# Which engine copies the transposed attention weights out of PSUM: a transformer layer with a 1024-token sliding window on eight NeuronCores

## The chip, the cores and the metric

One Trainium2 chip (trn2), all eight NeuronCores, one program on each. The metric is the device time in microseconds of the slowest core, as the median of several executions. Two batches of 4096 tokens are split into eight pieces of 1024 tokens; each core computes its own piece and reads another 1024 tokens in front of it (the halo) for keys and values. There is no exchange between cores. Engines are called PE (matmul), ACT (ScalarE), DVE (VectorE), POOL (GpSimd, which here only issues the casting DMAs) and SP.

## What is computed

The reference, cut to what matters:

```python
# attention: 32 query heads, 8 kv heads, head size 128, window 1024
q = rope(x @ wq); k = rope(x @ wk); v = x @ wv
scores = einsum('bqhgd,bshd->bhgqs', q, k) * 128 ** -0.5
scores = where((j <= i) & (j > i - 1024), scores, neg)
attn   = softmax(scores)
x = layernorm(x + einsum('bhgqs,bshd->bqhgd', attn, v) @ wo)
# ffn: dense 4096x4096 plus bias, plus the LoRA rank picked per token by a gate
x = layernorm(x + x @ W.T + b + lora(x))
```

## The kernel before, in words

The program of a core goes through four stages, in this order: keys and values of 2048 tokens (L382 and its helpers); then twice (`NPASS`, two passes of 512 tokens) the attention of all 32 heads followed by the output projection, the first layer norm and a transposition (L739 to L798); then the dense layer of the ffn (L939 and after). All matmuls are bf16.

`Prog.do` records one group of instructions for one engine and derives its waits from `Res` objects: a resource remembers the last writer's token (`w`) and the readers since (`r`). A read waits for `w`; a write waits for `w` and for every reader. Each engine executes its own list strictly in the order in which the program text recorded it. Nothing is reordered later.

The attention of one pass walks over heads h and, inside a head, over four query blocks s4 of 128 rows. A query block looks at KW = 1152 keys (nine blocks of 128). One block, called a step below, is spread over three turns of the loop:

- `emit_C` (L599 and after): the scores on PE, in three pieces of 512, 512 and 128 columns (all L613) with two mask matmuls (L618, L622), into three PSUM banks: 0 to 2 or 3 to 5 by the parity of the step.
- `emit_post`: one exp over the 1152 columns on ACT (L628, whose accumulator is read by a second instruction), then on DVE the sum's correction (L632), the reciprocal (L635) and the scaling of the probabilities `pb` (L637).
- `tailT`, one turn later: nine PE transposes of `pb`. Eight go to bank 6 (L647), the ninth (L654) into the free end of the third score bank of this step's parity. Then two copies bring them to SBUF as `pts`: eight blocks in one copy of 1024 columns (L658), the ninth in a copy of 128 columns (L663). Both declare `r_pts` as written.
- `tailA`, one turn after that: nine matmuls of V against `pts` (L676), whose 128x128 result ACT copies away (L681).

Between these stands `emit_A_piece`: eight of the 32 matmuls that project the next head's queries (L554, bank 7). At the end of a head `emit_B` turns the projected queries into rotated ones: ACT copies bank 7 to `qraw` (L565), PE multiplies by a permutation (L568), DVE does two products and a sum (L575, L578, L581). The first score matmul of the next head needs the result.

A turn of the loop thus reads: scores of i, `tailA` of i-2, projection piece, exp and scaling of i, `tailT` of i-1. After the last head, `tailsA` and `tailsT` are emptied, and the loads of the residual rows (`xo`) and of the output weights (`wo_r`) feed the next stage; the `xo` loads are released by the last projection piece.

```python
                    post, tT, tA = emit_C(h, s4)
                    if len(tailsA) >= 2:
                        tailsA.pop(0)()
                    if h + 1 < HQ:
                        emit_A_piece(h + 1, s4, QS)
                    post()
                    if tailsT:
                        tailsT.pop(0)()
```

Of the kernel before, what the change touches and what calls it, by code (L numbers as in the profile page):

```python
# [9 lines left out]
AF = mybir.ActivationFunctionType  # L10
# [144 lines left out]
def build_program(cfg):  # L155
# [36 lines left out]
    with contextlib.ExitStack() as es:  # L192
# [75 lines left out]
        def bankb(i):  # L268
            return PSb[:, i * 1024:(i + 1) * 1024]

        P = Prog(nc, es)
# [206 lines left out]
        for p_i in range(NPASS):  # L478
# [105 lines left out]
            def emit_C(h, s4):  # L584
# [55 lines left out]
                def tailT(h=h, s4=s4, sg=sg, hk=hk, pb=pb, rp=rp,  # L640
                          av_bk=t9_bk, av_off=av_off):
                    nfull = KW // 128
                    pts = scr.bf(PTS, KW)
                    n6 = min(8, nfull)
                    fns = []
                    for j in range(n6):
                        fns.append(lambda e, j=j, pb=pb: e.transpose(  # L647
                            bankb(6)[:, j * 128:(j + 1) * 128],
                            pb[:, j * 128:(j + 1) * 128], c_id[:, :]))
                    extra = []  # L650
                    for j in range(n6, nfull):
                        xoff = 2 * (av_off + 128) + (j - n6) * 128
                        extra.append(xoff)
                        fns.append(lambda e, j=j, pb=pb, xoff=xoff, av_bk=av_bk: e.transpose(  # L654
                            bankb(av_bk)[:, xoff:xoff + 128],
                            pb[:, j * 128:(j + 1) * 128], c_id[:, :]))
                    P.do("pe", fns, reads=[rp] + RC, writes=[r_bank[6], r_bank[av_bk]])
                    P.do("dve", lambda e, pts=pts, n6=n6: e.tensor_copy(  # L658
                        pts[:, 0:n6 * 128], bankb(6)[:, 0:n6 * 128]),
                        reads=[r_bank[6]], writes=[r_pts])  # L660
                    if nfull > n6:
                        P.do("dve", lambda e, pts=pts, n6=n6, nfull=nfull, av_bk=av_bk,
                             x0=extra[0]: e.tensor_copy(  # L663
                            pts[:, n6 * 128:nfull * 128],
                            bankb(av_bk)[:, x0:x0 + (nfull - n6) * 128]),
                            reads=[r_bank[av_bk]], writes=[r_pts])

                def tailA(h=h, s4=s4, sg=sg, hk=hk,
# [4 lines left out]
                    for j in range(nfull):  # L673
# [10 lines left out]
                        AF.Copy),  # L684
                        reads=[r_bank[av_bk]], writes=[r_D])
                return emit_post, tailT, tailA

            emit_A_load(0)
# [455 lines left out]
```

How the kernel before makes its waits and increments, by code:

```python
    def _wait(self, q, tok):  # L81
        if tok is None:
            return
        pq, v = tok
        if v <= 0 or self.known[q].get(pq, 0) >= v:
            return
        sem = self.semh[pq]
        self.items[q].append(lambda e, sem=sem, v=v: e.wait_ge(sem, v))
        self.known[q][pq] = v
# [28 lines left out]
        def wrapped(e, fn=last, sem=sem, step=step):  # L118
            fn(e).then_inc(sem, step)
# [35 lines left out]
def build_program(cfg):  # L155
# [640 lines left out]
                    dap = z1buf[:, :].rearrange("p (c t) -> p c t", t=PT)[  # L796
                        :, dc0:dc0 + len(chunks), ts * 128:(ts + 1) * 128]
                    P.do("dve", lambda e, bk=bk, dap=dap, n=len(chunks): e.tensor_copy(
                        dap, bankb(bk)[:, 0:n * 128].rearrange("p (c t) -> p c t", t=128)),
                        reads=[r_bank[bk]], writes=[rz1])
        if cfg.get("DEBUG_Z1") or cfg.get("DEBUG_PRE"):
            for ry in r_y:
                if ry.dmasem is not None:
                    ysem = P.semh[ry.dmasem]
                    P.raw("sdma", lambda e, ysem=ysem, v=P.cnt[ry.dmasem]: e.wait_ge(ysem, v))
            return _finish(nc, P, es)
        cA = a2.bf(0, DC * MAXR)
        cB_off = DC * MAXR
# [172 lines left out]
                    emit_ln2(t8w)  # L982
        for ry in r_y:
            ysem = P.semh[ry.dmasem]
            final_cnt = P.cnt[ry.dmasem]
            P.raw("sdma", lambda e, ysem=ysem, v=final_cnt: e.wait_ge(ysem, v))
        return _finish(nc, P, es)
```

## Time and profile before

| what | value |
|---|---|
| median of 3 runs | 3679.27 us (3673.71 to 3823.28) |
| the profiled execution's own time | 3675.64 us |
| span of its slowest core (core 4) | 3674.1 us |
| spans of the eight cores | 3651.0 to 3674.1 us |
| mean granted TensorE clock, share of full speed | 0.891 on core 4 |
| PE, DVE, ACT busy, share of the span | 72%, 24%, 14% |
| first L568 to last L568 of the two passes' heads 1 to 31 | 686.1 to 1322.9 us and 1760.7 to 2396.1 us |

Times in rows count from the span's start. The span is first to last instruction on one core; the execution's own time is 1.5 us longer. "Idle before" is attributed by the profile to what released the engine.

### The profile page before, as it was taken

The page shows a single profiled execution, that of the slowest core. Times are in us where ns is not written, and L with a number is a line of the kernel's source. Part 1 is how long each engine was busy: PE and PEld are TensorE (multiplying, and loading weights), DVE is VectorE, ACT ScalarE, POOL GpSimd, SP SyncE. Part 2 cuts the span into 40 slices and gives each one's busy share as a digit, 9 for nine tenths or more (in the row PEclk, how much of TensorE's full clock was granted, in tenths as well). Part 3 has the DMA queues.
Part 4 walks back from the last instruction along what each step waited for, and adds up shares of the span by engine and source line. Part 5 has one row for each costly group of instructions (what it writes and reads, how often), then busy time and mean ns, then how long its engine had stood idle before and what let it go on. Part 6 is the DMA issues. An engine that isn't in the chain of part 4 may idle for free.

```text
span 3674.1 us, 40837 instructions; the slowest of 8 cores (3651.0 to 3674.1 us)
## 1 busy us (share of the span) xinstructions
PE 2644.7 (72%) x15313; PEld 1331.2 (36%) x15602; DVE 876.1 (24%) x2156; ACT 510.6 (14%) x934; POOL 225.0 (6%) x295
## 2 busy tenths in 40 slices
PE   4888888776667667775776676767774777767774
PEld 2343443444444433333444444433332333323332
DVE  1111111233333321112333333311112111111111
ACT  0000000222233210001332322210001000010001
POOL 1000000000000000000000000000000000000000
PEclk8899999999999988887999999978886888878887
DMA  8777876422322357773323223276762366685665
GB/s 129 126 133 132 147 129 126 78 50 47 54 51 47 55 85 101 101 103 51 55 47 58 47 47 55 38 115 92 107 100 35 48 92 91 91 171 82 91 91 137
DMA packets 177542, 315.36 MB, mean 86 GB/s; under 512 B 5688, under 2 KB 136904, under 8 KB 176328
## 3 DMA queue, kind: packets, MB, share of 16 engines
q0 software_dynamic: 175824, 295.89, 51.7%
q1 hardware_dynamic: 1528, 16.85, 1.2%
q8 instruction: 130, 2.13, 0.2%
q14 instruction: 60, 0.49, 0.0%
HBM read 591.81 MB, written 16.78 MB: 166 GB/s over the span
## 4 chain that ended last, share of the span: by engine, by line
PE 41%; DMA 21%; DVE 16%; issue 10%; ACT 9%; DVEq 1%; ACTq 0%; POOL 0%; POOLq 0%; SPq 0%
PE PS L739 11%; PE PS L939 11%; ACT SCR L628 8%; PE PS L382 7%; DMA SCR<-wo_r 6%; DMA SCR<-W_r 5%; DMA SCR<-wk_l 5%; DVE SCR L658 5%; DMA SCR<-wv_l 4%; PE PS L676 4%; PE PS L613 2%; PE PS L554 2%; DVE SCR L663 1%; DVE B L970 1%; DVE B L747 1%
## 5 line engine op out<-in xcount | busy, mean ns | idle before, releaser
L739 PE MATMUL PS<-SCR,B 128*128 128x512 bf16 x2006 | 505.6, 415 | 166.3 <-DVE B L747 81.8
L939 PE MATMUL PS<-SCR,B 128*128 128x512 bf16 x2000 | 511.3, 420 | 124.4 <-DMA SCR<-W_r 82.6
L382 PE MATMUL PS<-B,SCR 128*128 128x512 bf16 x2010 | 478.4, 396 | 93.7 <-DMA SCR<-wv_l 46.0
L554 PE MATMUL PS<-B,SCR 128*128 128x512 bf16 x1948 | 492.9, 397 | 4.5 <-PE PS L676 0.9
L613 PE MATMUL PS<-B,SCR 128*128 128x512 bf16 (+1 forms) x716 | 208.2, 334 | 371.1 <-DVE SCR L663 213.0
L739 PEld LDWEIGHTS PS<-SCR,B 128*128 128x128 bf16 x2048 | 212.7, 105 | 458.7 <-issue 261.0
L939 PEld LDWEIGHTS PS<-SCR,B 128*128 128x128 bf16 x2048 | 214.3, 106 | 418.0 <-issue 226.0
L382 PEld LDWEIGHTS PS<-B,SCR 128*128 128x128 bf16 x2048 | 203.9, 101 | 354.3 <-issue 142.8
L628 ACT ACTIVATE SCR<-PS 128x1152 bf16<-128x1152 f32 x256 | 289.3, 1130 | 11.0 <-PE PS L622 8.0
L554 PEld LDWEIGHTS PS<-B,SCR 128*128 128x128 bf16 x2048 | 197.4, 102 | 201.0 <-issue 32.0
L613 PEld LDWEIGHTS PS<-B,SCR 128*128 128x128 bf16 x768 | 73.9, 100 | 473.1 <-issue 445.2
L632 DVE TENSOR_TENSOR sumt<-sums,c_corr 128x1 f32<-128x1 f32 x256 | 40.7, 159 | 720.6 <-ACT SCR L628 720.6
L681 ACT ACTIVATE B<-PS 128x128 bf16<-128x128 f32 x256 | 70.9, 277 | 937.2 <-PE PS L676 937.2
L676 PE MATMUL PS<-SCR,B 128*128 128x128 bf16 x2304 | 180.6, 226 | 7.2 <-DVE SCR L663 7.1
L747 DVE TENSOR_TENSOR B<-PS,B 128x512 bf16<-128x512 f32 x64 | 44.3, 692 | 592.0 <-PE PS L739 586.3
L658 DVE COPY SCR<-PS 128x1024 bf16<-128x1024 bf16 x256 | 174.9, 683 | 23.4 <-PE PS L654 23.1
L967 DVE COPY SCR<-PS 128x512 bf16<-128x512 bf16 x64 | 26.3, 411 | 625.4 <-PE PS L960 625.4
L647 PE MATMUL PS<-c_id,SCR 128*128 128x128 bf16 x2048 | 160.8, 223 | 7.6 <-ACT B L681 5.7
L647 PEld LDWEIGHTS PS<-c_id,SCR 128*128 128x128 bf16 x2048 | 139.8, 100 | 69.7 <-issue 14.6
L676 PEld LDWEIGHTS PS<-SCR,B 128*128 128x128 bf16 x2304 | 143.6, 101 | 10.0 <-issue 8.7
L637 DVE TENSOR_SCALAR SCR<-SCR,rcp 128x1152 bf16<-128x1152 bf16 x256 | 134.3, 525 | 28.8 <-DVE rcp L635 2.0
L309 POOL DMA_DIRECT2D SCR<-wq_l x64 | 44.9, 702 | 1279.9 <-PE PS L654 1183.1
(91 smaller groups left out, 1469.9 us busy)
## 6 DMA issues: line engine op xcount, KB each, us to landing
SCR<-wq_l POOLq DMA_DIRECT2D x64, 1024.0 KB, 9.1
SCR<-wo_r POOLq DMA_DIRECT2D x64, 1024.0 KB, 10.3
SCR<-W_r POOLq DMA_DIRECT2D x64, 1024.0 KB, 10.1
SCR<-wk_l POOLq DMA_DIRECT2D x32, 1024.0 KB, 9.6
SCR<-wv_l POOLq DMA_DIRECT2D x32, 1024.0 KB, 9.4
B<-xo POOLq DMA_DIRECT2D x16, 1024.0 KB, 14.5
y<-B SPq DMA_DIRECT2D x8, 2048.0 KB, 8.1
B<-xh POOLq DMA_DIRECT2D x8, 1024.0 KB, 16.9
```

The costliest lines, as they stand in the source:

```text
L382: fns.append(lambda e, kc=kc, wsl=wsl, pjb=pjb, g=g: e.matmul(PS[:, pjb * 512: pjb * 512 + GRP], wsl[:, kc * 128:(kc + 1) * 128], xg_ap(g, ...
L554: fns.append(lambda e, kc=kc, wsl=wsl, xfm_ap=xfm_ap: e.matmul(PS[:, 7 * 512: 7 * 512 + PT], wsl[:, kc * 128:(kc + 1) * 128], xfm_ap(kc), ...
L613: e.matmul(PS[:, bkk * 512: bkk * 512 + wdt], qrot[:, s4 * 128:(s4 + 1) * 128], B3[:, hk * EXT + elo + off: hk * EXT + elo + off + wdt], s ...
L628: P.do("act", lambda e, bs=bs, pb=pb: e.activation(pb[:, 0:KW], PS[:, bs * 512: bs * 512 + KW], AF.Exp, accum_out=sums3[:, 0:1]), reads=sb ...
L637: P.do("dve", lambda e, pb=pb: e.tensor_scalar_mul(pb, pb, rcp[:, :]), reads=[rp, r_rcp], writes=[rp])
L647: fns.append(lambda e, j=j, pb=pb: e.transpose(bankb(6)[:, j * 128:(j + 1) * 128], pb[:, j * 128:(j + 1) * 128], c_id[:, :]))
L658: P.do("dve", lambda e, pts=pts, n6=n6: e.tensor_copy(pts[:, 0:n6 * 128], bankb(6)[:, 0:n6 * 128]), reads=[r_bank[6]], writes=[r_pts])
L676: e.matmul(PS[:, av_bk * 512 + av_off: av_bk * 512 + av_off + 128], vview[:, kt, hk, :], pts[:, j * 128:(j + 1) * 128], start=(j == 0), st ...
L681: P.do("act", lambda e, DBt=DBt: e.activation(DBt[:, h * PT + s4 * 128: h * PT + (s4 + 1) * 128], PS[:, av_bk * 512 + av_off: av_bk * 512 ...
L739: fns.append(lambda e, ts=ts, kc=kc, wch=wch, kcl=kcl, DBt=DBt: e.matmul(bank(ts), DBt[:, kc * PT + ts * 128: kc * PT + (ts + 1) * 128], w ...
L747: P.do("dve", lambda e, ts=ts, xres_sl=xres_sl: e.tensor_add(xres_sl, bank(ts), xres_sl), reads=[r_bank[ts], r_xres], writes=[r_xres], ext ...
L939: fns.append(lambda e, tj=tj, t8=t8, dc=dc, wch=wch, dcl=dcl: e.matmul(bank(tj), z1_ap(dc, t8 * 128, 128), wch[:, dcl * 512:(dcl + 1) * 51 ...
```

## The change

The copy of the eight transposed blocks, L658, is recorded for ACT as an activation with function Copy where it was a `tensor_copy` on DVE. Its source, its destination and its declared reads and writes are the same, and so is its place in the text. The small copy of the ninth block, L663, stays on DVE.

```diff
                     P.do("pe", fns, reads=[rp] + RC, writes=[r_bank[6], r_bank[av_bk]])
-                    P.do("dve", lambda e, pts=pts, n6=n6: e.tensor_copy(
-                        pts[:, 0:n6 * 128], bankb(6)[:, 0:n6 * 128]),
+                    P.do("act", lambda e, pts=pts, n6=n6: e.activation(
+                        pts[:, 0:n6 * 128], bankb(6)[:, 0:n6 * 128], AF.Copy),
                         reads=[r_bank[6]], writes=[r_pts])
                     if nfull > n6:
                         P.do("dve", lambda e, pts=pts, n6=n6, nfull=nfull, av_bk=av_bk,
```

On DVE, around the end of a head, the kernel before has these rows (SCR holds `pb`, `pts` and the query scratch, PS is PSUM; `s_pe`, `s_act`, `s_dve` are the engines' counters):

```order
L637 TENSOR_SCALAR SCR<-SCR,rcp 128x1152 [waits s_dve]
L658 COPY SCR<-PS 128x1024 [waits s_pe]
L663 COPY SCR<-PS 128x128 [waits s_dve]
L575 TENSOR_TENSOR SCR<-PS,c_sin 128x512 [waits s_pe]
L578 TENSOR_TENSOR SCR<-SCR,c_cos 128x512 [waits s_act,s_dve]
L581 TENSOR_TENSOR SCR<-SCR 128x512 [waits s_dve]
```

The same place on DVE in the changed kernel:

```order
L637 TENSOR_SCALAR SCR<-SCR,rcp 128x1152 [waits s_dve]
L663 COPY SCR<-PS 128x128 [waits s_pe,s_act]
L575 TENSOR_TENSOR SCR<-PS,c_sin 128x512 [waits s_pe]
L578 TENSOR_TENSOR SCR<-SCR,c_cos 128x512 [waits s_act,s_dve]
L581 TENSOR_TENSOR SCR<-SCR 128x512 [waits s_dve]
```

L658 has left the row, and L663, which waited for its own engine's copy before, now waits for PE's transposes and for ACT: both copies write `r_pts`, and the later one waits for the earlier one's token.

On ACT, at the end of a head, the kernel before has (B is the buffer of the attention's output, sums the accumulator):

```order
L681 ACTIVATE B<-PS 128x128 [waits s_pe,s_act]
L628 ACTIVATE SCR,sums<-PS 128x1152 [waits s_dve,s_act]
L565 ACTIVATE SCR<-PS 128x512 [waits s_pe]
L681 ACTIVATE B<-PS 128x128 [waits s_pe,s_act]
L628 ACTIVATE SCR,sums<-PS 128x1152 [waits s_dve,s_act]
```

The same place on ACT in the changed kernel:

```order
L681 ACTIVATE B<-PS 128x128 [waits s_pe,s_act]
L628 ACTIVATE SCR,sums<-PS 128x1152 [waits s_act,s_dve]
L658 ACTIVATE SCR<-PS 128x1024 [waits s_pe,s_dve]
L565 ACTIVATE SCR<-PS 128x512
L681 ACTIVATE B<-PS 128x128 [waits s_pe,s_act]
L628 ACTIVATE SCR,sums<-PS 128x1152 [waits s_act,s_dve]
L658 ACTIVATE SCR<-PS 128x1024 [waits s_pe,s_dve]
```

L658 now stands behind every exp. At the end of a head it also stands in front of L565, the copy with which the next head's queries begin. PE's rows are in the same order in both kernels.

## Rows read from the trace of the kernel before

**Rows 1.** The page: busy time, share of the span and instructions of each engine.
```profile
PE 2644.7 (72%) x15313; PEld 1331.2 (36%) x15602; DVE 876.1 (24%) x2156; ACT 510.6 (14%) x934; POOL 225.0 (6%) x295
```

**Rows 2.** Waits, 683 to 1323 us: total us, times, longest.
```profile
PE PS L613 <- DVE SCR L663: 100.4, 90, 1.7
PE PS L613 <- DVE SCR L581: 73.5, 30, 2.9
```

**Rows 3.** Timeline, one step inside a head: start, us, engine, line, operation.
```profile
950.43 0.66 PE L676 MATMUL PS<-SCR,B 128*128 128x128 bf16 x9
951.25 0.28 ACT L681 ACTIVATE B<-PS 128x128 bf16<-128x128 f32 x1 [3.17 <-PE PS L676]
...
952.47 0.19 ACT L628 ACTIVATION_READ_ACCUMULATOR SCR<-PS 128x1 f32 x1
...
953.11 0.22 PE L654 MATMUL PS<-c_id,SCR 128*128 128x128 bf16 x1
...
953.30 0.52 DVE L637 TENSOR_SCALAR SCR<-SCR,rcp 128x1152 bf16<-128x1152 bf16 x1
...
953.74 0.68 DVE L658 COPY SCR<-PS 128x1024 bf16<-128x1024 bf16 x1
954.52 0.23 DVE L663 COPY SCR<-PS 128x128 bf16<-128x128 bf16 x1
...
954.89 0.22 PE L613 MATMUL PS<-B,SCR 128*128 128x128 bf16 x1 [1.08 <-DVE SCR L663]
...
955.02 0.27 PE L676 MATMUL PS<-SCR,B 128*128 128x128 bf16 x2
```

**Rows 4.** Lines by form, ACT, 683 to 1323 us: count | busy us, mean ns | idle before.
```profile
L628 ACT ACTIVATE SCR<-PS 128x1152 bf16<-128x1152 f32 x121 | 136.7, 1130 | 1.4 <-ACT B L681 1.4
L681 ACT ACTIVATE B<-PS 128x128 bf16<-128x128 f32 x121 | 33.5, 277 | 442.9 <-PE PS L676 442.9
```

**Rows 5.** Timeline, the end of a head and the start of the next.
```profile
1004.65 0.60 ACT L565 ACTIVATE SCR<-PS 128x512 bf16<-128x512 f32 x1 [0.25 <-remote]
...
1004.83 0.22 PE L654 MATMUL PS<-c_id,SCR 128*128 128x128 bf16 x1
...
1005.50 0.38 PE L568 MATMUL PS<-SCR,c_p 128*128 128x512 bf16 x1 [0.45 <-ACT SCR L565]
1006.25 0.23 DVE L663 COPY SCR<-PS 128x128 bf16<-128x128 bf16 x1
1006.39 0.68 DVE L575 TENSOR_TENSOR SCR<-PS,c_sin 128x512 bf16<-128x512 f32 x1
...
1008.27 0.59 PE L613 MATMUL PS<-B,SCR 128*128 128x512 bf16 x1 [2.40 <-DVE SCR L581]
```

**Rows 6.** Timeline, PE alone, a head's first step.
```profile
986.34 0.38 PE L613 MATMUL PS<-B,SCR 128*128 128x512 bf16 x1 [2.40 <-DVE SCR L581]
...
986.93 0.67 PE L676 MATMUL PS<-SCR,B 128*128 128x128 bf16 x9
...
991.29 0.22 PE L654 MATMUL PS<-c_id,SCR 128*128 128x128 bf16 x1
...
992.90 0.27 PE L676 MATMUL PS<-SCR,B 128*128 128x128 bf16 x2
```

**Rows 7.** Windows in that step: length, busy PE, PEld, DVE, ACT, POOL; PEclk, DMA, GB/s.
```profile
987.70:991.00 3.30, 3.30 (x11) 1.38 (x11) 0.84 (x3) 1.42 (x3) 0.00 (x0) 0.50 0.85 170
```

**Rows 8.** Timeline, L568: heads 1 and 31, pass one; heads 1 and 31, pass two.
```profile
686.09 0.38 PE L568 MATMUL PS<-SCR,c_p 128*128 128x512 bf16 x1 [0.44 <-ACT SCR L565]
1322.90 0.38 PE L568 MATMUL PS<-SCR,c_p 128*128 128x512 bf16 x1 [0.45 <-ACT SCR L565]
1760.72 0.38 PE L568 MATMUL PS<-SCR,c_p 128*128 128x512 bf16 x1 [0.45 <-ACT SCR L565]
2396.12 0.38 PE L568 MATMUL PS<-SCR,c_p 128*128 128x512 bf16 x1 [0.45 <-ACT SCR L565]
```

**Rows 9.** Timeline, PE, the first matmuls of the first output projection.
```profile
1356.49 1.49 PE L739 MATMUL PS<-SCR,B 128*128 128x512 bf16 x3 [3.87 <-DMA SCR<-wo_r]
```

## The prediction

> **What bounds the kernel now.** I read the page's engine shares first: PE is busy 72% of the span, DVE 24%, ACT 14% [rows 1]. No helper engine is full, so what counts is not how much work the copy is but whether somebody waits for it. The list of waits of the first pass answers that: PE's score matmul L613 waited 100.4 us in 90 waits for DVE's small copy L663, and 73.5 us in 30 waits for L581, the last operation of the query rotation [rows 2]. So attention is a chain across engines, in which both copies stand.
>
> The timeline of one step inside a head shows its order. The nine V matmuls L676 start at 950.43; the last transpose L654 ends at 953.11 + 0.22 = 953.33, that is 2.90 us later, PE working throughout. L658 could start then, but DVE is still scaling (L637 until 953.82), so it starts at 953.74. L663 ends at 954.75, the last score piece starts at 954.89 and the next L676 at 955.02 [rows 3]. One step is 4.59 us: 2.90 of PE work and 1.69 from the last transpose to the next L676.
>
> At the end of a head L565 runs on ACT beside the transposes. The last transpose ends at 1005.05, L568 starts at 1005.50, and the next head's first score matmul at 1008.27, 3.22 us after the transposes; L575, at 1006.39, is released by DVE getting through with L663 and not by L568, which was done at 1005.88 [rows 5]. From the first score matmul to L676 it takes 0.59 us at full clock [rows 6]. So that step is 2.90 + 3.22 + 0.59 = 6.71 us, and a head without disturbance 3 x 4.59 + 6.71 = 20.48 us. The measured mean from L568 to L568 is larger: (1322.90 - 686.09) / 30 = 21.23 and (2396.12 - 1760.72) / 30 = 21.18 us [rows 8].
>
> Of the 0.73 us between, part is the clock. After some head changes PE, having done nothing but L568 for 3.22 us, works at a granted clock of 0.50, which is 1.2 of 2.4 GHz [rows 7]. In such a head L676 to the last transpose takes 991.51 - 986.93 = 4.58 us in place of 2.90; the next L676 then follows only 1.39 us behind, since L637 is long done [rows 6]. The head loses 5.97 - 4.59 = 1.38 us, and 0.30 of the clock's 1.68 us are swallowed by the wait for DVE. At 1.38 us each, not more than about half of the heads can be such. I take 0.4 of them, which leaves 0.18 us for small delays.
>
> **The change, part by part.**
>
> *The copy's own duration.* The profile has no ACT copy with a 16-bit source in PSUM. The nearest rows are ACT's reads of fp32 from PSUM: 1130 ns for 1152 columns, 277 ns for 128 [rows 4], so 0.833 ns a column, and 1023 ns for 1024 columns. Above, 1.13 us bounds it, as the larger instruction takes that. Below, 0.60 us bounds it: L565 reads the same 2 KB of a partition in that time [rows 5], if bytes and not columns set the pace. I take 1.02 us, because column count explains all three ACT rows (512 columns give 597 ns). On DVE it was 0.68.
>
> The Trainium skill's page "VectorE: DVE Perf Modes", section "The TRN2 errata", has a table that gives ScalarE reading PSUM 172 + FD/Accel cycles at 1.2 GHz. With Accel 1 my estimate from it is 1.00 us, with Accel 2, which the table leaves possible for bf16, 0.57 us; no row here decides between the two.
>
> *Who waits for it inside a head.* ACT is free: exp's accumulator read ends at 952.66, 0.67 us ahead of the last transpose [rows 3]. ACT answers PE in 0.16 us (L676 ends at 951.09, L681 starts at 951.25 [rows 3]). DVE's scaling is no longer in front of the copy, which would be a gain of 0.41 - 0.16 = 0.25 us. But L663 did not become free: it writes `r_pts` too and so waits for ACT's token. From the last transpose: 0.16, copy 1.02, 0.10 to DVE (the gap between L658 and L663 today; I take it for the hop from ACT too), L663 0.23, and 0.27 from its end to L676 (954.75 to 955.02) [rows 3]. That is 1.78 us where it was 1.69. The step becomes 2.90 + 1.78 = 4.68, 0.09 more, and its third score piece still waits for L663.
>
> *At the end of a head.* L565 stood beside the transposes and now stands behind the copy in ACT's queue. From the last transpose: 0.16, copy 1.02, L565 0.60, 0.25 to L568 (1005.25 to 1005.50), L568 0.38, 0.15 to L575, and 1.88 from L575 to the first score matmul [rows 5]: 4.44 us where it was 3.22. Queued behind the waiting L565 is ACT's next L681, which is needed later anyway; DVE's L575 waits for PE now and not for DVE. The step becomes 2.90 + 4.44 + 0.59 = 7.93 us. An undisturbed head is 3 x 4.68 + 7.93 = 21.97 us, 1.49 more.
>
> *The clock.* The stretch in which PE has only L568 to do grows from 3.22 to 4.44 us. Today fewer than half of the heads fall to 0.50 behind it; how the share grows, no row says. It lies between no change (0.4) and all heads; I take nearly all. And nothing swallows part of the loss any more: in a slow step the copy already waits for the transposes in every step, so the whole 1.68 us count. That is 0.4 x 1.68 = 0.67 us a head at the low end, 1.68 at the high end; I take 1.45. The Trainium skill's page "TensorE: Matmul & The Clock Gate", section "Loop structure matters more than you think", says that a long wait between matmuls makes the next ones run cold. By that rule every head would be cold, which would put the sum 14 us higher; the trace so far agrees with it for some heads only.
>
> *The sum.* The new mean head is 21.97 + 1.45 = 23.42 us; the small delays of today are mostly late L637s, now off the path. Against 21.20 that is 2.22 us. It counts in 30 heads of each pass: what lies behind the last L568 is covered, since the output projection starts only when its weights land, 3.87 us after PE could [rows 9], and these loads are released by the last projection piece, ahead of the longer rotation. 60 x 2.22 = 133 us. The profiled execution took 3675.6 us; the sum gives 3809. The median of the runs is 3.6 us above that execution, so I say 3810, 3.5% slower. The other stages have none of these instructions; at their work of 3 ms I cost the change nothing.
>
> **The rivals.**
>
> *A. The clock share stays as it is.* For it: the drop is not tied to every gap, and a gap of 3.22 us often passes. Against: the gap grows by 1.22 us around an unchanged L568. A head is 21.97 + 0.67 = 22.64, and 60 x 1.44 = 86 us: 3762.
>
> *B. ACT copies 16-bit data twice as fast, and the kernel is not slower.* It decides at ACT's reading of bank 6. With a copy of 0.60 each of the four hops of a head is 0.42 shorter: 21.97 - 1.68 = 20.29 us undisturbed, below today's 20.48. With the clock share as it is, 20.29 + 0.67 = 20.96, and 60 x -0.24 = -14: 3661. With nearly all heads at half clock, 21.74 and 3708. The point from which it decides, with today's share, is 21.20 = 20.96 + 4 x (copy - 0.60), a copy of 0.66 us. Against: the three ACT rows lie on one line of columns. This is the case of the page's table with Accel 2.
>
> *C. The change lets L663 go ahead, so that ACT only delays L676.* Then a step would be 2.90 + 0.16 + 1.02 + 0.25 = 4.33 us and a head 20.92 undisturbed; with 1.45 for the clock 22.37, so 60 x 1.17 = 70 us: 3746. Against it stands the order, in which L663 waits for `s_act`; for it only that this wait might be met early, which the sequence excludes.
>
> *D. It costs more.* A copy of 1.13 adds 4 x 0.11 = 0.44 us, all heads at half clock another 0.23: 24.09, 60 x 2.89 = 173, 3849.
>
> **How the numbers follow.** The forecast has 0.66, A 0.16, B 0.08, C 0.03, D 0.07. A measurement of this kernel can tell about 2%, 3753 us here, from no change. Slower than that are the forecast, D and most of A: 0.85. Within 2% are C, the rest of A and most of B: 0.13. Faster by 2% (3606) is beyond even B's better form: 0.02. The range for 8 in 10 runs from just under A, 3748, to just under D, 3845.
>
> **What would show each step.** In the changed trace: L658 on ACT, 1.02 us long, 0.16 us behind L654. L663 starts about 0.1 us behind its end, and PE's wait inside a head still carries L663's name. L676 to L676 is 4.68 us in undisturbed steps. L568 starts about 2.0 us after the last transpose (0.45 today), and the first score matmul 4.4 us after it. The stretches behind it show a clock of 0.50 in nearly every head, and the mean from L568 to L568 is 23.4 us. I am wrong if L658 takes 0.6 us, if PE does not wait for L663, or if most heads begin at full clock.

## The result, and the profile after

The changed kernel takes 3831.76 us (median of 9 runs) against 3681.57 us; the ratio is 1.0409, 95% interval 1.0397 to 1.0422. The forecast was 3810 us, range 3748 to 3845, slower. In some executions of any of these kernels the cores of a die run at a lower clock throughout; the ratios leave those out, and where a kernel below has no ratio, too few others were left for one, so their times are given.

The page of the changed kernel, engine shares:

```profile
PE 2741.6 (72%) x15602; PEld 1355.9 (35%) x15602; DVE 725.4 (19%) x1900; ACT 758.4 (20%) x1190; POOL 225.3 (6%) x295
```

ACT rose from 14% to 20% and DVE fell from 24% to 19% [rows 1]; neither is near full, before or after. Matmul busy time rose by 97 us though the matmuls are the same: in part they ran at the lower clock, in part some of their records are missing from the trace before.

The lines by form of the changed kernel, 687 to 1403 us (count | busy us, mean ns | idle before), give the copy's own duration:

```profile
L658 ACT ACTIVATE SCR<-PS 128x1024 bf16<-128x1024 bf16 x120 | 122.9, 1024 | 144.3 <-PE PS L654 142.5 <-DVE rcp L635 1.8
```

1024 ns, where 1023 were worked out from the fp32 copies [rows 4]. In this copy ACT took as long per column for 16-bit PSUM data as for fp32.

The waits of the changed kernel, 683 to 1400 us (total us, times, longest), to be held against [rows 2]:

```profile
ACT SCR L658 <- PE PS L654: 142.5, 117, 2.5
DVE SCR L663 <- ACT SCR L658: 139.5, 120, 2.5
PE PS L613 <- DVE SCR L663: 104.4, 90, 1.2
...
PE PS L613 <- DVE SCR L581: 60.8, 30, 2.4
PE PS L568 <- ACT SCR L565: 57.5, 30, 1.9
```

The first three lines are the new chain: PE's transposes release ACT's copy, the copy releases L663, and L663 releases PE. The wait under L663's name is as large as before, so the copy that left DVE has not left the path. The last line is new in this size: PE waited 0.45 us for L565 at the end of a head [rows 5] and now waits 1.9 us.

The timeline of one step inside a head, changed kernel, which answers to [rows 3]:

```profile
750.81 0.22 PE L654 MATMUL PS<-c_id,SCR 128*128 128x128 bf16 x1
...
751.18 1.02 ACT L658 ACTIVATE SCR<-PS 128x1024 bf16<-128x1024 bf16 x1 [0.84 <-PE PS L654]
752.31 0.23 DVE L663 COPY SCR<-PS 128x128 bf16<-128x128 bf16 x1 [0.81 <-ACT SCR L658]
752.68 0.22 PE L613 MATMUL PS<-B,SCR 128*128 128x128 bf16 x1 [1.16 <-DVE SCR L663]
...
752.80 0.66 PE L676 MATMUL PS<-SCR,B 128*128 128x128 bf16 x9
```

The transposes end at 751.03 and L676 starts 1.77 us later (1.69 before, 1.78 forecast). Each link can be read off: 0.15 to ACT, 1.02, 0.11 to DVE, 0.23, 0.26 to L676.

The end of a head in the changed kernel, which answers to [rows 5]:

```profile
755.48 0.22 PE L654 MATMUL PS<-c_id,SCR 128*128 128x128 bf16 x1
...
755.85 1.02 ACT L658 ACTIVATE SCR<-PS 128x1024 bf16<-128x1024 bf16 x1 [0.84 <-PE PS L654]
756.77 0.59 ACT L565 ACTIVATE SCR<-PS 128x512 bf16<-128x512 f32 x1
756.98 0.23 DVE L663 COPY SCR<-PS 128x128 bf16<-128x128 bf16 x1 [0.81 <-ACT SCR L658]
757.61 0.38 PE L568 MATMUL PS<-SCR,c_p 128*128 128x512 bf16 x1 [1.91 <-ACT SCR L565]
758.09 0.69 DVE L575 TENSOR_TENSOR SCR<-PS,c_sin 128x512 bf16<-128x512 f32 x1 [0.89 <-PE PS L568]
...
759.99 0.38 PE L613 MATMUL PS<-B,SCR 128*128 128x512 bf16 x1 [2.00 <-DVE SCR L581]
```

L565 starts 0.10 us before the copy's recorded end (756.87). L568 comes 1.91 us after the last transpose (0.45 before), the next head's first score matmul 4.29 us after it (3.22 before, 4.44 forecast). DVE's L575 is now released by PE and not by DVE's own queue.

What follows the longer gap is seen in windows of one such place and of the next head change, changed kernel (length, busy PE, PEld, DVE, ACT, POOL; PEclk, DMA, GB/s):

```profile
755.70:760.00 4.30, 0.39 (x2) 0.14 (x3) 2.23 (x5) 1.51 (x2) 0.70 (x1) 1.00 0.64 103
760.00:767.00 7.00, 5.84 (x38) 3.10 (x39) 1.07 (x4) 2.41 (x4) 0.00 (x0) 0.76 0.44 89
...
779.20:783.50 4.30, 0.41 (x2) 0.16 (x3) 2.21 (x5) 1.51 (x2) 0.71 (x1) 0.80 0.63 98
784.20:788.20 4.00, 4.00 (x19) 2.14 (x18) 0.59 (x3) 1.39 (x3) 0.00 (x0) 0.50 0.62 126
```

In both gaps PE works for 0.4 of 4.3 us. Behind the first, part of the next 7 us ran at 0.50; at the second the clock fell inside the gap already and all of the 4 us behind it were at 0.50, or 1.2 GHz. The clock in the trace shows half clock behind the head change in all 60 heads: 34 have the first form, in which the clock falls 0.1 to 1.3 us, mostly 1.2, after PE is back at work, and 26 the second, mostly every other head. What each costs is seen from L568 to L568 (PE, changed kernel):

```profile
781.09 0.38 PE L568 MATMUL PS<-SCR,c_p 128*128 128x512 bf16 x1 [1.92 <-ACT SCR L565]
805.36 0.38 PE L568 MATMUL PS<-SCR,c_p 128*128 128x512 bf16 x1 [1.92 <-ACT SCR L565]
```

The head that begins at 757.61, with the first form, took 23.48 us; the next, with the second, 24.27 us.

The mean head comes from L568 of heads 1 and 31, as in [rows 8]:

```profile
687.10 0.38 PE L568 MATMUL PS<-SCR,c_p 128*128 128x512 bf16 x1 [1.92 <-ACT SCR L565]
1402.78 0.38 PE L568 MATMUL PS<-SCR,c_p 128*128 128x512 bf16 x1 [1.92 <-ACT SCR L565]
1844.11 0.38 PE L568 MATMUL PS<-SCR,c_p 128*128 128x512 bf16 x1 [1.92 <-ACT SCR L565]
2559.98 0.38 PE L568 MATMUL PS<-SCR,c_p 128*128 128x512 bf16 x1 [1.92 <-ACT SCR L565]
```

23.86 us in both passes, against 21.23 and 21.18. The two stretches grew by 78.9 and 80.5 us, together 159 us; the profiled executions differ by 3831.84 - 3675.64 = 156 us. So the whole loss sits in these 60 heads; the rest of the program took 3 us less, which is within what single executions differ by. PE still waits for the output weights at the end of the first pass, so what lies behind the last L568 is covered by the DMA as assumed (PE, changed kernel; the wait was 3.87 us before [rows 9]):

```profile
1437.75 7.55 PE L739 MATMUL PS<-SCR,B 128*128 128x512 bf16 x28 [7.42 <-DMA SCR<-wo_r]
```

### The profile page after: what moved, and what is told of

The parts are those of the page before. It is cut to its first block, busy times and chain, and to the rows that moved or that the text cites. A ratio compares the mean times of both kernels' runs of the same rounds, so it can differ in the third digit from the quotient of the medians.

```text
span 3830.3 us, 41514 instructions; the slowest of 8 cores (3795.8 to 3830.3 us)
## 1 busy us (share of the span) xinstructions
PE 2741.6 (72%) x15602; PEld 1355.9 (35%) x15602; DVE 725.4 (19%) x1900; ACT 758.4 (20%) x1190; POOL 225.3 (6%) x295
## 4 chain that ended last, share of the span: by engine, by line
PE 55%; DMA 20%; ACT 9%; DVE 9%; issue 6%; DVEq 0%; POOL 0%; ACTq 0%; POOLq 0%; SPq 0%
PE PS L554 14%; PE PS L739 10%; PE PS L939 10%; PE PS L382 7%; ACT SCR L658 7%; DMA SCR<-wo_r 6%; DMA SCR<-W_r 5%; DMA SCR<-wk_l 4%; DMA SCR<-wv_l 4%; PE PS L676 4%; PE PS L647 3%; PE PS L613 2%; DVE B L970 1%; DVE B L747 1%; DVE SCR L575 1%
## 5 line engine op out<-in xcount | busy, mean ns | idle before, releaser
L554 PE MATMUL PS<-B,SCR 128*128 128x512 bf16 x2048 | 573.2, 431 | 0.0
L382 PE MATMUL PS<-B,SCR 128*128 128x512 bf16 x2048 | 476.3, 393 | 94.0 <-DMA SCR<-wv_l 49.3
L613 PE MATMUL PS<-B,SCR 128*128 128x512 bf16 (+1 forms) x768 | 228.3, 348 | 348.6 <-DVE SCR L663 219.3
L382 PEld LDWEIGHTS PS<-B,SCR 128*128 128x128 bf16 x2048 | 202.4, 101 | 356.0 <-issue 142.1
L658 ACT ACTIVATE SCR<-PS 128x1024 bf16<-128x1024 bf16 x256 | 262.2, 1024 | 298.8 <-PE PS L654 290.4
L554 PEld LDWEIGHTS PS<-B,SCR 128*128 128x128 bf16 x2048 | 212.3, 109 | 238.6 <-issue 98.1
L613 PEld LDWEIGHTS PS<-B,SCR 128*128 128x128 bf16 x768 | 75.3, 102 | 461.0 <-issue 434.4
L676 PE MATMUL PS<-SCR,B 128*128 128x128 bf16 x2304 | 190.3, 233 | 7.1 <-DVE SCR L663 7.1
L676 PEld LDWEIGHTS PS<-SCR,B 128*128 128x128 bf16 x2304 | 152.1, 105 | 10.8 <-issue 8.0
```

Source lines behind the costliest of these rows:

```text
L382: fns.append(lambda e, kc=kc, wsl=wsl, pjb=pjb, g=g: e.matmul(PS[:, pjb * 512: pjb * 512 + GRP], wsl[:, kc * 128:(kc + 1) * 128], xg_ap(g, ...
L554: fns.append(lambda e, kc=kc, wsl=wsl, xfm_ap=xfm_ap: e.matmul(PS[:, 7 * 512: 7 * 512 + PT], wsl[:, kc * 128:(kc + 1) * 128], xfm_ap(kc), ...
L613: e.matmul(PS[:, bkk * 512: bkk * 512 + wdt], qrot[:, s4 * 128:(s4 + 1) * 128], B3[:, hk * EXT + elo + off: hk * EXT + elo + off + wdt], s ...
L658: P.do("act", lambda e, pts=pts, n6=n6: e.activation(pts[:, 0:n6 * 128], bankb(6)[:, 0:n6 * 128], AF.Copy), reads=[r_bank[6]], writes=[r_pts])
L676: e.matmul(PS[:, av_bk * 512 + av_off: av_bk * 512 + av_off + 128], vview[:, kt, hk, :], pts[:, j * 128:(j + 1) * 128], start=(j == 0), st ...
```

## The experiments

The forecast's theory is three terms: a step inside a head is little longer, the end of a head is longer because L565 queues behind the copy, and the longer quiet stretch brings the half clock. The rival behind all of them is the plain one: a 1.02 us copy in place of a 0.68 us one costs its difference wherever it stands. Twelve runs follow, in four groups; one kernel was run twice. An undisturbed head means, as in the prediction, one at full clock throughout and without small delays; it is added up from the parts of such a head. Line numbers in their rows are their own.

### Where in the head the cost arises

**e2_headend_dve**, three copies of four on ACT, and **e3_headend_act**, only the copy ahead of `emit_B` on ACT (for the latter the condition is `s4 == QS - 2`):

```diff
+                    if s4 != QS - 2:
+                        P.do("act", lambda e, pts=pts, n6=n6: e.activation(
+                            pts[:, 0:n6 * 128], bankb(6)[:, 0:n6 * 128], AF.Copy),
+                            reads=[r_bank[6]], writes=[r_pts])
+                    else:
+                        P.do("dve", lambda e, pts=pts, n6=n6: e.tensor_copy(
+                            pts[:, 0:n6 * 128], bankb(6)[:, 0:n6 * 128]),
+                            reads=[r_bank[6]], writes=[r_pts])
```

Expected of e2_headend_dve:

> The changed kernel, but the copy recorded right in front of emit_B (one of four in a head) is back on DVE. Theory (the head change carries the cost, three steps add only 0.08 us each): steps 4.67, the head change back at 6.71 us, half clock behind it about as often as in the kernel before; a head is 0.2 to 0.4 us longer than before, so 3690 to 3705. Rival (each copy on ACT costs about the same): three quarters of the 150 us stay, 3795.

Expected of e3_headend_act:

> The kernel before, with only the copy right in front of emit_B on ACT. Theory: steps 4.59, the head change 7.8 us, half clock behind nearly every one, a head about 23.3 us against 21.2: 3800, between 3785 and 3820. Rival (each copy costs the same): one quarter of 150 us, 3720.

e3_headend_act: ratio 1.0429 (1.0371 to 1.0486) to the kernel before. One copy of four makes all of the loss; the rival's quarter is excluded. It was slower than my upper bound, though. The windows of its heads 1 to 31 in one pass:

```profile
690.86:1406.35 715.49, 497.04 (x3678) 291.43 (x3751) 231.00 (x660) 214.79 (x420) 21.54 (x31) 0.86 0.24 43
```

30 heads in 715.49 us are 23.85 each, the same as with all four copies moved, although the undisturbed parts (3 x 4.59 and 7.79) sum to 21.56. The second form of the half clock stands here in 28 of 30 heads, where the changed kernel has it in 13 of 30. The mean clock is 0.86, lower than the changed kernel's 0.90 over the same heads.

e2_headend_dve missed: it took 3750 and 3759 us, between the two theories. Its undisturbed parts are as forecast (steps 4.67, head change 6.68, sum 20.69), but the mean head is 22.16 us. The cores of this one execution are far apart:

```profile
core 1: 3757.4 us, clock 0.862
...
core 6: 3669.5 us, clock 0.891
```

All cores run the same instructions, and the slower ones have the lower clock. The 0.2 us by which the undisturbed head grew cannot be what costs 80 us; the clock was the candidate, and the runs below test it.

Not all of the 80 us belongs to the heads. On core 1 the two stretches of heads grew by 28 and 33 us against the kernel before, and 18 us more lie between the two passes, 455.4 against 437.8 us. For 193 us of that stretch the granted clock of this core stood at 0.81; three more of the eight cores show 0.81 somewhere in this execution, and none in the profiled execution of the kernel before (core 1):

```profile
1498.20:1515.20 17.00, 14.27 (x55) 5.68 (x53) 2.25 (x4) 0.00 (x0) 1.75 (x2) 0.81 0.57 87
```

On core 1 this reaches into the first heads of the second pass too. The first pass, from which the 22.16 us are, is free of it on all cores.

### What the half clock is worth

**e4_fill** adds dummy matmuls to the changed kernel, whose result the next head's first score matmul overwrites:

```diff
+            def emit_fill(n):
+                bkf = 0 if qsc[0] % 2 == 0 else 3
+                P.do("pe", [lambda e, bkf=bkf: e.matmul(
+                    PS[:, bkf * 512: bkf * 512 + 512], c_id[:, :], c_cos[:, 0:512],
+                    start=True, stop=True)] * n,
+                    reads=RC, writes=[r_bank[bkf]])
...
+                if h > 0:
+                    emit_fill(7)
                 P.do("pe", lambda e, qraw=qraw: e.matmul(
...
+                if h > 0:
+                    emit_fill(6)
```

> The changed kernel with work added to PE alone: 7 dummy matmuls of 512 columns ahead of L568 and 6 behind it, into the bank that the next head's first score matmul overwrites, so they fill the quiet stretch and delay nobody at full clock. Theory (the quiet stretch is what brings the half clock behind it, worth 2.1 us a head): clock 1.0 behind the head change, a head 21.8 to 22.0 us, so about 3715 to 3725, faster than the changed kernel although PE does more. Rival (the half clock comes from something else, load or time): no gain, 3830 or more.

Ratio 1.0061 (1.0036 to 1.0087), median 3706.61 us: 125 us less than the changed kernel, by giving PE 13 useless matmuls a head. The end of a head shows them under L563:

```profile
756.82 1.46 PE L563 MATMUL PS<-c_cos,c_id 128*128 128x512 bf16 x6
756.92 1.02 ACT L669 ACTIVATE SCR<-PS 128x1024 bf16<-128x1024 bf16 x1 [0.84 <-PE PS L665]
757.84 0.59 ACT L572 ACTIVATE SCR<-PS 128x512 bf16<-128x512 f32 x1
...
758.69 0.38 PE L577 MATMUL PS<-SCR,c_p 128*128 128x512 bf16 x1 [0.41 <-ACT SCR L572]
758.90 1.46 PE L563 MATMUL PS<-c_cos,c_id 128*128 128x512 bf16 x6
...
761.18 0.38 PE L624 MATMUL PS<-B,SCR 128*128 128x512 bf16 x1 [0.82 <-DVE SCR L592]
```

The chain behind the copy (L572 is L565, L577 is L568) is the same up to L568; from there to the first score matmul it takes 2.49 us in place of 2.38. What changed is the clock; windows of heads 1 to 31:

```profile
692.93:1351.38 658.45, 516.64 (x4140) 295.75 (x4141) 174.37 (x570) 304.67 (x510) 21.58 (x31) 1.00 0.27 47
```

Clock 1.00 throughout and 658.45 / 30 = 21.95 us a head in place of 23.86. Nothing but what PE does in the quiet stretch was altered, so the quiet stretch brings the half clock.

The same filling was then put into the kernel before (**e7_before_fill**, 7 dummy matmuls behind L568, run twice), into e2_headend_dve (**e9_steps_fill**, the same 7) and into e3_headend_act (**e10_headend_fill**, 7 ahead and 6 behind).

> The kernel before with 7 dummy matmuls of 512 columns behind L568, in the quiet stretch of the head change. Theory (the 0.73 us by which today's mean head exceeds the undisturbed one is mostly half clock): clock 1.0 behind every head change, a head 20.5 to 20.7 us against 21.2, so 30 to 40 us less: 3640 to 3650. With e4_fill it gives the price of the change without the clock, about 60 us. Rival: the kernel before loses little to the clock, 3675 or more.

> e7_before_fill again, for its interval: 3630 to 3640 by its first profile, 1.1 to 1.4% under the kernel before.

> e2_headend_dve (three of four copies on ACT, the one at the head's end on DVE) with 7 dummy matmuls behind L568. Theory (clean sums): 3 x 4.67 + 6.7 = 20.7 us a head with no half clock, 0.2 above e7_before_fill, so about 10 to 15 us over it: 3645 to 3655. That the plain e2_headend_dve was far above this is then all half clock. Rival (three copies on ACT cost more than their steps show): over 3680.

> e3_headend_act (only the copy at the head's end on ACT) with 7 dummy matmuls ahead of L568 and 6 behind it. Theory: 3 x 4.59 + 7.9 = 21.7 us a head and no half clock, 15 us under e4_fill: about 3690. Rival (the head change costs what e3_headend_act showed, clock or not): 3800 or more.

The four kernels, with and without filling; the head is the mean over heads 1 to 31 of the first pass, on the slowest core of the profiled execution:

| copies on ACT | head, plain | head, filled | filled kernel against the kernel before |
|---|---|---|---|
| none | 21.23 us | 20.83 us | no ratio; 3633 to 3642 us |
| three inside the head | 22.16 us | 20.89 us | 0.9859 (0.9831 to 0.9886) |
| the one at the head's end | 23.85 us | 21.77 us | 1.0012 (0.9987 to 1.0037) |
| all four | 23.86 us | 21.95 us | 1.0061 (1.0036 to 1.0087) |

In the filled column the terms add up to within 0.12 us, which they do not in the plain one. The three inner copies cost 0.06 us a head (0.08 each was read from the step; some of the fixed delays of the kernel before go with it), the one at the end 0.94, all four 1.12. All four filled kernels are a little worse at the head change than their plain forms: the first score matmul comes 3.37 us behind the last transpose in place of 3.22 (none), 3.31 for 3.19, 4.41 for 4.30 and 4.41 for 4.30. That is 0.11 to 0.15 us in each filled row, so it nearly drops out of the differences. e10_headend_fill and e7b_before_fill came out as expected; e7_before_fill ended at or under the low end of its expectation, e4_fill and e9_steps_fill some 10 to 20 us under theirs, none near its rival's.

### Which waits carry the rest

**e1_split** gives the ninth block a resource of its own:

```diff
+        r_pts9 = Res()
...
-                            reads=[r_bank[av_bk]], writes=[r_pts])
+                            reads=[r_bank[av_bk]], writes=[r_pts9])
...
-                    P.do("pe", fns, reads=[r_pts, r_vtm], writes=[r_bank[av_bk]])
+                    P.do("pe", fns, reads=[r_pts, r_pts9, r_vtm], writes=[r_bank[av_bk]])
```

> The changed kernel with a resource of its own (r_pts9) for the ninth block, so that L663 no longer waits for ACT's copy; L676 reads both. Theory (inside a head the copy reaches PE through ACT, then DVE's L663, then PE): without the L663 link a step goes from 4.67 to about 4.33 us (0.16 + 1.02 + 0.25 behind the last transpose), the head change stays at 7.8 us, a head loses 1.0 us, 60 heads 61 us: about 3770, between 3755 and 3785. Rival (the link through L663 is covered by something else, the copy itself is what PE waits for): steps stay at 4.67 and the time at 3830.

Ratio 1.0227 (1.0165 to 1.0289), median 3766 us, inside the expectation. One step of it:

```profile
776.44 0.22 PE L655 MATMUL PS<-c_id,SCR 128*128 128x128 bf16 x1
...
776.81 1.02 ACT L659 ACTIVATE SCR<-PS 128x1024 bf16<-128x1024 bf16 x1 [0.81 <-PE PS L655]
...
777.26 0.21 DVE L664 COPY SCR<-PS 128x128 bf16<-128x128 bf16 x1
777.62 0.22 PE L614 MATMUL PS<-B,SCR 128*128 128x128 bf16 x1 [0.48 <-DVE SCR L664]
...
777.98 0.66 PE L677 MATMUL PS<-SCR,B 128*128 128x128 bf16 x9
```

The small copy and the third score piece now run while ACT copies, and the V matmuls start 1.32 us after the last transpose (776.66 to 777.98) in place of 1.77; the step is 4.21 us. From the copy's end (777.83) to PE it takes 0.15 us, not the 0.25 I had read from L565 to L568.

**e5_l565_first** records L565 right after the exp of the turn that ends a head, ahead of `tailT`; **e6_split_l565** is that with e1_split's resource.

```diff
                     post()
+                    if s4 == QS - 1 and h + 1 < HQ:
+                        emit_B0(h + 1)
                     if tailsT:
```

(`emit_B0` holds the ACT copy of `emit_B`; the rest stays in its place.)

> The changed kernel with L565 recorded ahead of the transposes' copy on ACT in the turn that ends a head. Theory (the head change is longer because L565 queues behind the copy): L568 again 0.45 us behind the last transpose, but DVE's L575 now stands behind L663, which waits for ACT's copy (0.60 + 1.02 + 0.1 + 0.2), so the first score matmul comes about 3.35 us behind the last transpose (4.30 in the changed kernel, 3.22 before). Undisturbed head 20.8 us; with a half-clock loss of 0.7 to 1.9 us a head 3695 to 3765. Rival (the order on ACT at the head's end is not the cause): 4.3 us and 3830.

> Both repairs: L565 ahead of the copy and r_pts9 for the ninth block. Theory: steps 4.21 us as in e1_split, first score matmul 2.86 us behind the last transpose, undisturbed head 3 x 4.21 + 6.34 = 18.97 us, 1.5 under the kernel before. The half clock decides how much stays: at 0.7 to 2.1 us a head 19.7 to 21.1, so 3590 to 3675. Rival (ACT's 1.02 us copy costs by itself): not under 3680.

e5_l565_first: ratio 1.0190 (1.0122 to 1.0258). The end of a head:

```profile
742.71 0.60 ACT L564 ACTIVATE SCR<-PS 128x512 bf16<-128x512 f32 x1 [0.28 <-PE PS L554]
...
743.27 1.02 ACT L662 ACTIVATE SCR<-PS 128x1024 bf16<-128x1024 bf16 x1
743.56 0.38 PE L572 MATMUL PS<-SCR,c_p 128*128 128x512 bf16 x1 [0.44 <-ACT SCR L564]
744.39 0.22 DVE L667 COPY SCR<-PS 128x128 bf16<-128x128 bf16 x1 [0.81 <-ACT SCR L662]
744.53 0.68 DVE L579 TENSOR_TENSOR SCR<-PS,c_sin 128x512 bf16<-128x512 f32 x1
...
746.42 0.38 PE L617 MATMUL PS<-B,SCR 128*128 128x512 bf16 x1 [2.49 <-DVE SCR L585]
```

PE's L572 (L568) is early again, but DVE does not use it: L579 (L575) stands behind L667 (L663), which waits for the copy. The first score matmul is 3.30 us behind the last transpose: the 4.30 of the changed kernel is gone, by exactly one of its two ties. e6_split_l565 cuts the other as well: 2.83 us, a head of 20.44 us, ratio 0.9897 (0.9836 to 0.9958), its profiled execution 3623.82 us. With the same copy on the same engine the kernel is now 1% faster than before; the interval is clear of 1, and the gain is small.

### An attempt on the length of the head

e2_headend_dve has the gap of the kernel before (first score matmul 3.19 us behind the last transpose, 3.22 before), but half clock behind 25 and 24 of 30 head changes where the kernel before has 13 and 12. Windows of heads 1 to 31 in the first pass, the kernel before and then e2_headend_dve:

```profile
686.08:1322.90 636.82, 445.93 (x3679) 268.88 (x3751) 245.02 (x692) 188.50 (x390) 20.31 (x30) 0.97 0.27 49
691.96:1356.80 664.84, 474.74 (x3751) 277.61 (x3751) 189.49 (x602) 277.77 (x480) 20.35 (x30) 0.93 0.27 47
```

In the first pass all eight cores show it: 12 to 14 head changes with half clock before, 21 to 29 in e2_headend_dve. Either the 0.2 us in the head's length or the ACT copies in its steps had to be the reason. **e11_before_longer** was to lengthen the head alone:

```diff
+                    if s4 == 0:
+                        P.do("dve", lambda e: e.memset(idxf[:, :], 0.0), writes=[r_gate])
```

> The kernel before with one tiny DVE memset (128x1) between L658 and L663 in one step of a head: that step grows by about 0.2 us, ACT has no copy, and the gap at the head's end is unchanged. Theory (how often the half clock follows the gap depends on the length of the whole head, which is why e2_headend_dve lost 80 us with 0.2 us more): half clock behind 18 to 29 of 30 head changes in place of 13, a mean head of 21.8 to 22.4 us, 3720 to 3760. Rival (the copies on ACT inside the head brought it): 0.2 us a head and nothing more, 21.4 us and 3690.

Ratio 0.9979 (0.9943 to 1.0015), a head of 21.26 and 21.07 us on the slowest core, half clock behind 13 and 10 of 30 head changes. By the times the rival would seem to win, but the kernel did not do what it was built for. DVE's timeline around the memset:

```profile
693.58 0.68 DVE L658 COPY SCR<-PS 128x1024 bf16<-128x1024 bf16 x1
694.21 0.06 DVE L662 MEMSET idxf<- 128x1 f32 x1
694.37 0.23 DVE L665 COPY SCR<-PS 128x128 bf16<-128x128 bf16 x1
```

The small copy starts 0.79 us after the large one's start; without a memset it is 0.78 [rows 3]. The memset fitted into the gap that the semaphore between the two copies leaves, so the head was not longer and the run says nothing on its length.

### The version that beats both

**e8_split_l565_fill** is e6_split_l565 with 6 dummy matmuls behind L568.

> e6_split_l565 with 6 dummy matmuls behind L568. Theory: undisturbed heads of 19.0 to 19.2 us in nearly all, 60 x -2.05 = -123 us against the kernel before: 3550 to 3575. Rival (the half clock behind the head change is not from the quiet stretch when heads are this short): no better than e6_split_l565.

Ratio 0.9653 (0.9603 to 0.9704), median 3564.26 us. Windows of its heads 1 to 31:

```profile
700.60:1274.10 573.50, 483.27 (x3931) 275.97 (x3932) 164.03 (x571) 309.95 (x511) 20.29 (x30) 1.00 0.34 54
```

19.12 us a head at full clock.

## Why the prediction was right, point by point

**The copy's duration** (1.02 us by columns, 0.60 by bytes): 1.024. This settled rival B, and with it the sign. The faster of the two readings of the Trainium skill's table (page "VectorE: DVE Perf Modes", section "The TRN2 errata", Accel 2, 0.57 us) is excluded by that row; Accel 1 gives 1.00, and the row agrees.

**Inside a head** (+0.09 us a step, because L663 waits for ACT): 4.67 against 4.59 us, and e1_split showed the link by cutting it. Rival C, in which L663 goes ahead, was rightly excluded from the order of the waits; e1_split is what C would have needed in the source.

**At the head's end** (7.93 us): 7.78. I counted 0.15 too much: ACT starts L565 0.10 us before the copy's recorded end, and DVE's L575 follows L568 by 0.10 us (757.99 to 758.09) where I took 0.15. The hop from L565 to L568 is 0.25 us, as assumed. An undisturbed head was 3 x 4.67 + 7.78 = 21.79, not 21.97 us. That it is the order on ACT was shown by e5_l565_first and e6_split_l565.

**The clock** (1.45 us a head, at most 1.68): this is the term that was mis-sized. The measured head is 23.86 - 21.79 = 2.07 us above the undisturbed one. The direction was right, that nearly all heads would fall to half clock: in the profiled execution all 30 of each pass did. The upper bound was wrong. I had taken the one form that I saw, a half-clock stretch that costs 1.68 us, as the most a head can lose. For 34 of the 60 heads that price holds (23.48 - 21.79 = 1.69 us); the other 26 have a half-clock stretch that begins inside the gap and lasts until the transposes of the next step (the windows from 779.20 on), and the one shown loses 24.27 - 21.79 = 2.48 us. Rival A, the clock share as before, is excluded.

**The sum.** Two errors of opposite sign, -0.18 in the undisturbed head and +0.62 in the clock, make the difference between 23.42 and 23.86 us, that is 26 us in 60 heads; the forecast was 22 us low. That it came so near is in part luck, since the clock term alone was 37 us short. The 60 heads and the cover behind the last one held.

**How the 150 us divide.** Filled against filled, 1.12 us a head or 67 us are the longer chain; by the undisturbed heads it is 21.79 - 20.48 = 1.31 us or 79 us, and the difference is mostly small delays, which the filled kernel before has (20.83 us on average, 20.61 in its quickest head) and e4_fill hardly has (21.95 and 21.89). The rest is clock: filling gains 125 us in the changed kernel (3831.76 to 3706.61) and about 45 in the kernel before (3681.57 to 3637). The direct cost of the longer chain is thus about half of what the change costs.

What stays open is what sets the share of heads that fall to half clock. It is not the gap alone: e2_headend_dve has the gap of the kernel before and twice its share, and e6_split_l565 has the shortest gap of all, 2.83 us, and half clock behind 29 of 30 head changes in each pass. That the period of the whole head matters is my reading, since e2_headend_dve's head is 0.21 us longer, and since e3_headend_act with shorter steps lost more to the clock than the changed kernel with the same gap. It was argued and not shown: the one run made for it, e11_before_longer, did not lengthen the head. A simple rule by which a longer head falls more often does not fit e6_split_l565, whose undisturbed head is 1.5 us shorter than the one before. The rival, that ACT copies inside the steps raise the share, was not excluded: e2_headend_dve, e5_l565_first and e6_split_l565 have them and lie at 23 to 29 of 30, the kernel before and e11_before_longer have none and lie at 10 to 13. A gap of 4.30 us is enough without them: e3_headend_act has no ACT copy inside its steps and half clock behind all 30.

## What to carry to other kernels

Before moving an operation to an idle engine, read what stands behind it in that engine's queue and who shares its resource in the source: here the copy itself cost 0.34 us more, while the query copy queued behind it and the small copy tied to it by a shared resource set the price, and undoing both ties turned the same move into a gain. Where PE falls to half clock behind a gap, compare variants with the gap filled: there the terms add, and without filling a 0.2 us change in the period can look like one of 0.9. Filling such a gap with dummy matmuls is itself worth trying.

## What the runs showed of the hardware that I had not expected

- Useless matmuls make this kernel faster: 13 of 512 columns a head took the changed kernel from 3831.76 to 3706.61 us, 7 a head took the kernel before from 3681.57 to 3633 to 3642 us. The Trainium skill's page "TensorE: Matmul & The Clock Gate", section "Loop structure matters more than you think", says that a long DMA wait between matmuls leaves the next ones cold. Here the waits are for ACT and DVE; by that rule filling should help, and the runs agree, with the granted clock over heads 1 to 31 going from 0.90 to 1.00.
- A gap in which PE worked for 0.4 of 4.3 us was followed by half clock in every head of the changed kernel; the clock fell 0.1 to 1.3 us behind the gap's end in 34 heads and already inside it in 26.
- A 59 ns DVE memset between two copies tied by a semaphore cost nothing: the later copy started 0.79 us after the earlier one's start in place of 0.78.
- Cores with the same program and the same undisturbed steps ended 88 us apart in one execution of e2_headend_dve (3669.5 to 3757.4 us), with clocks of 0.891 and 0.862. Of the 88 us, 19 lie in the heads; the rest lies outside them, and 25 of it between the passes, where the slower core's clock showed 0.81.
